# Projection groups of eight token blocks over two PSUM banks, with the mask product of three of four groups on GpSimd

## What is computed

```python
def layer(x, mask, ...):                     # x: 1, 256, 256, 64
    xn = layernorm(_gn(x), norm_w, norm_b)
    left  = (xn @ w_left  + b) * sigmoid(xn @ w_lgate + b) * mask
    right = (xn @ w_right + b) * sigmoid(xn @ w_rgate + b) * mask
    out = einsum('bikh,bjkh->bijh', left, right)      # layers 0 and 2
    # layers 1 and 3 sum over the first token axis: 'bkjd,bkid->bijd'
    out = layernorm(out, onorm_w, onorm_b)
    return x + (out * sigmoid(xn @ w_ogate + b)) @ w_out
```

## Time and profile before

| | us |
|---|---|
| median of 3 runs | 2286.74 |
| lowest and highest of them | 2277.12, 2287.24 |
| the profiled execution | 2283.2 |
| its span | 2281.3 |
| PE busy in it | 1972.7 (86%) |
| DVE busy | 1766.1 (77%) |
| ACT busy | 1654.8 (73%) |
| POOL busy | 605.9 (27%) |

### The profile page before, as it was taken

How to read it: one execution, slowest core, us unless ns; L and a number is a source line. 1 busy time by engine, 2 the same in 40 slices (tenths; PEclk the granted TensorE clock), 3 DMA queues, 4 the chain that set the end, 5 groups by cost and what they waited for, 6 DMA issues and landing times. The chain is left out here.

```text
span 2281.3 us, 48887 instructions
## 1 busy us (share of the span) xinstructions
PE 1972.7 (86%) x13892; PEld 1408.9 (62%) x13892; DVE 1766.1 (77%) x2907; ACT 1654.8 (73%) x2597; POOL 605.9 (27%) x564
## 2 busy tenths in 40 slices
PE   4599887759899898969889899897988989898898
PEld 3433767636433788955443498885553359797565
DVE  5678899979768887869758897877985888787554
ACT  2388788859878877749878785765655878585566
POOL 0000546435310000015420080640652000000575
PEclk8699988969999999989999999998998999999899
DMA  8879949579979837498969993939997985667996
GB/s 323 322 226 271 278 114 272 159 256 416 373 218 280 298 126 266 152 350 352 420 253 283 268 248 107 281 100 375 392 421 243 281 295 166 225 218 261 370 420 276
DMA packets 484453, 624.77 MB, mean 274 GB/s; under 512 B 16496, under 2 KB 376944, under 8 KB 467952
## 3 DMA queue, kind: packets, MB, share of 16 engines
q1 hardware_dynamic: 482032, 606.61, 78.1%
q10 hardware_dynamic: 2304, 16.78, 1.8%
HBM read 413.61 MB, written 209.72 MB: 273 GB/s over the span
## 5 line engine op out<-in xcount | busy, mean ns | idle before, releaser
L733 PE MATMUL bank<-whigh,obuf 128*128 128x128 f16 x4096 | 507.2, 227 | 66.0 <-DMA obuf<-XH 28.6
L733 PEld LDWEIGHTS bank<-whigh,obuf 128*128 128x128 f16 x4096 | 466.4, 125 | 72.1 <-issue 55.3
L733 PE MATMUL bank<-wlow,obuf 128*128 128x128 f16 x4096 | 506.4, 227 | 0.4 <-issue 0.4
L733 PEld LDWEIGHTS bank<-wlow,obuf 128*128 128x128 f16 x4096 | 467.0, 125 | 1.6 <-issue 1.6
L867 PE MATMUL bank<-LR 128*128 128x256 f32 (+1 forms) x1792 | 375.5, 372 | 32.8 <-ACT obuf L879 16.9
L867 PEld LDWEIGHTS bank<-LR 128*128 128x128 f32 (+1 forms) x1792 | 320.3, 180 | 86.3 <-ACT obuf L879 23.4
L1186 POOL TENSOR_TENSOR LR<-LR,sum 128x2048 f32<-128x2048 f32 x32 | 145.7, 4552 | 550.9 <-DVE LR L1217 550.9
L755 ACT ACTIVATE sigs<-bank,small 128x256 f32<-128x256 f32 x512 | 238.1, 475 | 63.1 <-PE bank L733 56.0
L603 PE MATMUL bank<-LR,cen 128*128 128x512 f32 x512 | 256.4, 626 | 22.4 <-DMA LR<-XT 11.2
L655 DVE SCALAR_TENSOR_TENSOR LR<-bank,small,LR 126x1024 f32<-126x1024 f32 x128 | 164.3, 1284 | 121.0 <-ACT LR L636 120.6
L755 ACT ACTIVATE squares<-bank,small 128x256 f32<-128x256 f32 x512 | 237.4, 475 | 14.6 <-PE bank L733 8.1
(11 more groups left out here) (128 smaller groups left out, 3229.8 us busy)
## 6 DMA issues: line engine op xcount, KB each, us to landing
LR<-XT SPq DMA_DIRECT2D x128, 512.0 KB, 5.1
obuf<-XH SPq DMA_DIRECT2D x128, 512.0 KB, 6.2
LR<-XT SPq DMA_DIRECT2D x64, 1024.0 KB, 12.9
obuf<-XHA SPq DMA_DIRECT2D x128, 512.0 KB, 4.6
XT<-obuf SPq DMA_DIRECT2D x48, 1024.0 KB, 15.6
OS<-obuf SPq DMA_DIRECT2D x24, 2048.0 KB, 8.4
LR<-OS SPq DMA_DIRECT2D x96, 512.0 KB, 11.7
LR<-XH SPq DMA_DIRECT2D x64, 512.0 KB, 11.0
```

What stands on the lines that cost most here:

```text
L733: last = pe.matmul(bank(g)[:, j * P:(j + 1) * P], tokens, w[:, half * P:(half + 1) * P], start=part == 0, stop=part == 1)
```

## The change

A group becomes eight token blocks (sixteen matmuls) in a pair of PSUM banks. A chunk has four groups, and there are four bank pairs. The sigmoid, the mask product and the gated product each cover 512 elements per partition instead of 256, so there are half as many of them. `sig` and `msg` have four places of 512. The ring of TensorE is four groups deep instead of eight. In masked layers DVE makes the mask product of group 0 (directly ahead of the gated product of that same group), POOL those of groups 1, 2 and 3. SP's loads wait for the same chunk as before. The core of the diff:

```diff
+BY_VECTOR, BY_POOL = 0, (1, 2, 3)
...
-            by_vector, by_pool = (1, 5), (0, 2, 3, 4, 6, 7)
...
+            def pair(g):
+                return banks[g][:, :].rearrange("p (m c) -> p c m", m=8)
...
-                        for g in range(8):
-                            pe.wait_ge(products_ready.s, products_ready.n + 32 * i + 8 * h + g - 7)
-                            for j in range(4):
+                        for g in range(4):
+                            pe.wait_ge(products_ready.s, products_ready.n + 16 * i + 4 * h + g - 3)
+                            for j in range(8):
...
-                            act.activation(sig[g], bank(g).rearrange("p (m c) -> p c m", m=4)[:, C:, :],
-                                           ACT.Sigmoid, scale=unscale).then_inc(gates_ready.s, 1)
+                            act.activation(sig[g], pair(g)[:, C:, :], ACT.Sigmoid, scale=unscale) \
+                                .then_inc(gates_ready.s, 1)
...
-                            for g in by_pool:
+                            for g in BY_POOL:
...
-                                pool.wait_ge(products_ready.s, products_ready.n + group - 7)
+                                pool.wait_ge(products_ready.s, products_ready.n + group - 3)
                                 pool.tensor_tensor(msg[g], sig[g],
-                                                   mask_sb[:, kt, bass.ds(m, 4)].unsqueeze(1).broadcast_to([P, C, 4]),
+                                                   mask_sb[:, kt, bass.ds(m, 8)].unsqueeze(1).broadcast_to([P, C, 8]),
                                                    ALU.mult).then_inc(gates_masked.s, 1)
...
-                            if masked and g + 1 in by_vector:
...
-                                dve.tensor_tensor(msg[g + 1], sig[g + 1],
...
+                            elif g == BY_VECTOR:
+                                dve.wait_ge(gates_ready.s, gates_ready.n + group + 1)
+                                dve.wait_ge(products_ready.s, products_ready.n + group - 3)
+                                dve.tensor_tensor(msg[g], sig[g],
...
+                                dve.wait_ge(gate_masked_v.s, gate_masked_v.n + 4 * i + h + 1)
```

More of the change, by code:

```diff
@@ L147, in build @@
         rings = [[sb(f"{name}s", [P, 2 * BANK])[:, :], square[:, :]] for name, square in zip(("sig", "msg"), squares)]
-        sig, msg = ([v[:, i * 256:(i + 1) * 256].rearrange("p (c m) -> p c m", c=C) for v in ring for i in range(4)]
+        sig, msg = ([v[:, i * BANK:(i + 1) * BANK].rearrange("p (c m) -> p c m", c=C) for v in ring for i in range(2)]
                     for ring in rings)
@@ L709, in _ @@
                         n = 4 * i + h
-                        sp.wait_ge(projected.s, projected.n + 8 * n - 24)
+                        sp.wait_ge(projected.s, projected.n + 4 * n - 12)
                         sp.sem_inc(tick.s, 1)
@@ L780, in _ @@
                     for h in range(4):
-                        for g in range(8):
-                            group = 32 * i + 8 * h + g
+                        for g in range(4):
+                            group = 16 * i + 4 * h + g
                             kt, m = where(4 * i + h, g)
-                            if masked and g + 1 in by_vector:
-                                kt_v, m_v = where(4 * i + h, g + 1)
-                                dve.wait_ge(gates_ready.s, gates_ready.n + group + 2)
-                                dve.wait_ge(products_ready.s, products_ready.n + group - 6)
-                                dve.tensor_tensor(msg[g + 1], sig[g + 1],
-                                                  mask_sb[:, kt_v, bass.ds(m_v, 4)].unsqueeze(1).broadcast_to([P, C, 4]),
-                                                  ALU.mult).then_inc(gate_masked_v.s, 1)
@@ L800, in _ @@
+                            dve.scalar_tensor_tensor(dest[:, kt, :, bass.ds(m, 8)], pair(g)[:, 0:C, :],
                                                      unscale, gate[g], ALU.mult, ALU.mult) \
                                 .then_inc(products_ready.s, 1)
-            advance(*((landed[h], 8 * NCH) for h in range(4)), (projected, 8 * NCH), (gates_ready, 8 * NCH),
-                    (products_ready, 8 * NCH))
+            advance(*((landed[h], 8 * NCH) for h in range(4)), (projected, 4 * NCH), (gates_ready, 4 * NCH),
+                    (products_ready, 4 * NCH))
@@ L804, in project @@
             if masked:
-                advance((gates_masked, 6 * NCH), (gate_masked_v, 2 * NCH))
+                advance((gates_masked, 3 * NCH), (gate_masked_v, NCH))
         slot = lambda c: flat[:, c * COLS:(c + 1) * COLS]
```

38 lines of the change are left out of this document (18 added, 20 removed).

## The result

The changed kernel takes 2351.94 us in the median of 4 runs, against 2286.99 us for the kernel before, run beside it on the same chip: a ratio of 1.0297, 95% interval 1.0265 to 1.0329. (The ratio is taken over all runs; the quotient of the medians is 1.0284.) Slower, as forecast, but by 65 us and not by 50. The median lies at the very end of the range, 2352; on the 2286.7 of the forecast the ratio gives 2354.7 us, just above it. Of the ten executions of a later run (the wide form in the unmasked layers alone) one took 4918 us against some 2284 of the others; it is left out of that run's ratio, and nothing here shows its cause.

The account below looks back on a forecast made before the run. PE was taken to bound both kinds of half. Masked halves lose 48.4 us (13 intervals at 4.9 instead of 4.01 us, plus drains), unmasked drains 1.9: 50 us on 2283.2 gives 2333 us, range 2308 to 2352.

Parts of the forecast that it names:

- The place of the loss: Masked projection halves: PE is full at 4.01 us a chunk; cheaper DVE work buys nothing, the longer way round costs 48.4 us.
- The unmasked halves: Unmasked projection halves: no stall, since the way round is under 2 us of 2.7; only the drain grows, 1.9 us in four.
- The lock: Masked chunks: DVE's mask product waits up to 1.04 us for POOL's pair 1 product, once in two chunks, giving 5.04 us a chunk.
- the size of a masked chunk: Masked steady part: 4.9 us a chunk against 4.01, kept between 4.28 and 5.1.
- The count of 13 intervals: Masked half: from chunk 2 on, 13 chunk intervals are left to lose time, 13 x (4.9 - 4.01) = 11.6 us.
- The start: First chunks of a masked half: PE waits for transfers and runs at half clock, so the longer way round hides there.
- The drain: End of a masked half, where `contract` waits for the last product: 2.95 us before, +0.5 us after.
- No lock: Rival, masked chunks: DVE's mask product wins every time, queues alone decide, 4.5 us a chunk, 2312 us; chance 0.18.
- Not slower: Rival: POOL's price hangs on the broadcast mask's runs; at 0.84 us a product PE never waits, 2286 us; chance 0.06.
- Faster: Rival, masked halves: matmul spacing falls from 0.063 toward 0.0555 us, 29 us less, 2258 us; chance 0.03.
- The clock: Rival, masked halves: PE's idling lowers its clock, a chunk takes 6.9 us, 2380 to 2435 us; chance 0.08, shared with dearer POOL.
- A cheaper POOL: POOL's 512-wide mask product at the skill page's 1.11 us instead of 1.18: the sum some 20 us lower; no chance given.

## Where the prediction was right, and the step that failed

**The place of the loss: right.** PE's full steady part was the bound before, larger instructions on DVE and ACT bought nothing, and the masked halves carry 66.4 of the 66.4 us. The run without mask products (4.02 us a chunk) and the short ring of the kernel before (4.21 and 4.80) show the mechanism by itself.

**The unmasked halves: right.** +1.4 us where 1.9 was said, drains 0.48 us longer where 0.5 was said, and a ratio of 1.0002 when they alone are wide.

**The lock: right in its form, and by luck in its size.** One blocked chunk and one free one in turn, mask products of 0.69 and 1.72 us. "Carried on by hand" it gave 6.0 and 4.0 us; it is 6.5 and 4.1. The size of 1.04 us was 1.18 - 0.14, for a mask product that starts together with POOL's. It is 1.30 - 0.14 less the 0.12 by which DVE starts later, 1.04 again, and 1.72 - 0.68 is 1.04: POOL's higher price and the later start cancel.

**The step that failed: the size of a masked chunk, 4.9 us.** It measured 5.31. The loop itself holds. Its terms can be read off the trace from pair 1's last matmul to the same two chunks later; the last column is the mean of the five such loops with a locked mask product between chunks 4 and 14 of the first masked half:

| over two chunks, us | in the forecast | measured |
|---|---|---|
| pair 1's last matmul to POOL | 1.21 | 1.34 |
| three POOL products | 3.54 | 3.80 |
| POOL to product 3 | 0.15 | 0.14 |
| product 3 to mask product | 0.66 | 0.67 |
| mask product with its wait (the lock) | 0.69 + 1.04 | 1.74 |
| handoff to product 0 | 0.03 | 0.14 |
| product 0, and to TensorE | 0.75 + 0.05 | 0.75 + 0.06 |
| matmuls of pairs 0 and 1 | 1.95 | 2.00 |
| sum | 10.07 | 10.63 |
| a chunk | 5.04 | 5.32 |

(The rounded terms of the last column add up to 10.64.) The handoff inside DVE, from mask product to the gated product that needs it, is 260.81 - 260.67 = 0.14 us, in the free chunk 264.79 - 264.65 = 0.14 again. Four things made the 4.9. The sum of the locked loop, 5.04, was rounded down to 4.9 as if lock and queue overlapped, though in a serial loop every term counts: 0.14 a chunk. POOL's price was interpolated between 256 elements and 2048, from rows whose patterns differ, and the nearest row by size, 1.303 us for 512 elements, was set aside for its strides: wrong by 0.12 us, and 0.13 a chunk, since successive products start 1.25 us apart. The handoff was named "at most 0.15" and taken at 0.03: 0.055 a chunk. The rest, 0.09, is the way from pair 1 to POOL and a first matmul of a pair that takes longer. The upper end went the same way: 5.04 + 0.18 was cut to 5.1 "less the overlap", so that the locked case ended at 2344 us where 5.22 a chunk gives 2350. Nothing in the prediction derives the 2352 at which the range ended.

**The count of 13 intervals: about one too many.** From chunk 2's first matmul to the last matmul of the first half it was 56.7 us before and is 72.7 after, 16.0 more; the four masked halves have 16.0, 14.1, 14.7 and 16.1. 13 x 1.30 would be 16.9: the first intervals behind chunk 2 were above 4.0 us before as well (5.48 and 4.61 in the second half), so part of the loss is covered there. That error took off some of the too small chunk.

**The start: hidden in the first half only.** There the time to chunk 2 fell by 0.9 us (15.46 before, 14.52 after). In the other three masked halves it grew by 0.46, 0.53 and 1.95 us, which the forecast put at nothing.

**The drain: too low.** +0.87 us in the first half (327.57 - 323.75 = 3.82, against 2.95), where 0.5 was said; the prediction's own 3.3 + 0.3 - 2.95 is 0.65. POOL stands behind the lock and is 0.12 us a product dearer:

```profile
322.63 1.70 DVE L792 TENSOR_TENSOR msgs<-sigs,mask_sb 128x512 f32<-128x512 f32 x1
...
326.82 0.75 DVE L798 SCALAR_TENSOR_TENSOR LR<-bank,small,squares 128x512 f32 x1 [0.29 <-POOL squares L773]
```

The first half adds up: -0.9 + 16.0 + 0.9 is its 15.9 us within rounding. All four masked halves: 2.0 at the start, 60.9 behind it and 3.5 in the drains, 66.4 us, where the forecast had 0, 46.3 and 2.0.

**The rivals.** *No lock* is 4.79 us a chunk when made so, not 4.5: its sum had the same cheap POOL and handoff. The loop of that run measures 9.57 us, 3.80 of it for POOL's three products and 0.14 for the handoff, against the forecast's 9.03. *Not slower* asked for 0.84 us on POOL, which took 1.30; its idea that the broadcast's runs matter was right, but they cost here. *Faster* asked for a shorter matmul spacing, and it is 0.063 us as before (258.03, 258.09, 258.16). (Its 2258 us was counted from 2286.7; from the 2283.2 of the sum it is 2254.) *The clock*: granted 1.00 in the steady part with PE busy for 84% and idle up to 1.30 us at a time, as in the row with PE busy for 7.5 of 10 us. The page of the Trainium skill that spoke for a fall (TensorE: Matmul & The Clock Gate, "A second HAM failure mode: psum-queue depth-cycling") is not borne out in this kernel, though TensorE idles between groups as it cycles through PSUM. *A cheaper POOL*: the forecast put what a POOL product of 1.11 us would take off the sum at some 20 us. By its own hand count, 4.6 to 4.8 us a chunk for a POOL price below 1.16, it would be 5 to 16 us.

**What stays open.** The sixth half lost 19.0 us, 3 to 3.5 more than the others, at the same 5.28 us a chunk. 1.95 us of it lies before chunk 2, where TensorE's wait for a transfer grew:

```profile
1494.83 0.32 PE L736 MATMUL bank<-whigh,obuf 128*128 128x128 f16 x1 [6.49 <-DMA obuf<-XH]
```

Before it was 5.21 us. Why the transfer came later was not tested, nor why the starts of three masked halves grew.

## What to carry to other kernels

In a ring, an instruction twice as wide on fewer, larger places leaves the ring's time as it was and lengthens the way round, so a full engine can be made to wait without any engine being full: add up the way round, place by place, and compare it with the ring's time before joining two steps. Price an instruction by the row with its own pattern, or keep the dearer of two neighbours in the sum as well, and when a loop is serial, add its terms and subtract nothing for overlap. And where VectorE and GpSimd both multiply two SBUF operands, look for products whose length varies: ScalarE could leave one operand in PSUM here at no cost (0.66 against 0.69 us).

## What the runs showed of the hardware

- A DVE product of two SBUF operands waited for a GpSimd product until 0.14 us before its recorded end (258.83 + 1.30 against 258.95 + 1.72 - 0.68). A GpSimd product waited for DVE's likewise (1717 ns for 1300 behind the DVE product that ended at 260.67). With one operand in PSUM both waits are gone (682 ns, spread 14), and ACT's sigmoid of 512 elements takes 0.66 us within PSUM, 0.69 into SBUF.
- What a GpSimd product with a broadcast operand takes depends on the broadcast's pattern: 256 elements take 0.61 us in runs of four and 0.74 in runs of eight; 512 in runs of eight take 1.30. By the Trainium skill (GPSIMD Engine Reference, section 3.1), 512 elements would be an estimate of 1.11 us; the measured 1.30 decides.
- A DVE instruction that needs the result of the one right before it starts 0.14 us after that one's end (0.12 in layer 2); gated products of 256 elements that do not need it overlap the one before by 0.08 us.
